# Sparse graph attention with feed-forward: the software pipeline one step shorter, its lead-in written out, attention edges dealt by a computed pace

## What is computed

```python
hs, ht = layer_norm(x), layer_norm(h_target)            # scale and bias ln1
q = (ht @ Wq + bq) / sqrt(32);  k = hs @ Wk + bk;  v = hs @ Wv + bv
logits = where(adj != 0, q . k per head, -1e30)
ctx = softmax(logits) @ v                               # over the sources of each target
ht = layer_norm(ht + ctx @ Wo + bo)                     # scale and bias ln2
ff = gelu(ht @ W1) @ W2                                 # 256 -> 1024 -> 256
out = layernorm(x + ht + ff)                            # no scale
```

## Time and profile before

| | |
|---|---|
| median of 3 runs | 333.95 us (333.85 to 336.05) |
| profiled execution, its time | 333.58 us |
| its span in the profile | 331.8 us, 4310 instructions |
| PE busy | 250.6 us (76%) |
| DVE busy | 223.1 us (67%) |
| POOL busy | 186.1 us (56%) |
| ACT busy | 157.6 us (47%) |
| last third of it, chain that ended last | DVE and PE by turns |

### The profile page before, as it was taken

The page is one execution under the profiler, slowest core; times in us unless marked ns, Lnnn a source line. Parts: engine busy times, 40 slices in busy tenths (PEclk is TensorE's granted clock), DMA queues, the critical chain, the costliest instruction groups (busy, mean ns, idle before and its releaser), DMA issues.

```text
span 331.8 us, 4310 instructions
## 1 busy us (share of the span) xinstructions
PE 250.6 (76%) x1383; PEld 195.3 (59%) x1383; DVE 223.1 (67%) x623; ACT 157.6 (47%) x282; POOL 186.1 (56%) x204
## 2 busy tenths in 40 slices
PE   6599895650216745979999899899895796949990
PEld 6344331210112524967999799789784695939980
DVE  3489879798825437367897698688885589780111
ACT  1656999610014323465767567746752244303220
POOL 8776522390077765725777888887878603111211
PEclk9789979875555565979999999999999599787996
DMA  6999999999546645424346564454565700000000
GB/s 159 401 396 418 418 391 328 355 303 333 207 131 185 191 132 169 143 64 126 113 147 171 159 174 144 132 166 147 161 174 168 155 28 16 18 0 16 16 17 24
DMA packets 23490, 58.04 MB, mean 175 GB/s; under 512 B 4051, under 2 KB 12517, under 8 KB 21414
## 3 DMA queue, kind: packets, MB, share of 16 engines
q0 software_dynamic: 8400, 27.01, 28.1%
q1 hardware_dynamic: 14228, 29.91, 24.7%
q10 hardware_dynamic: 834, 0.79, 1.1%
HBM read 51.40 MB, written 10.49 MB: 187 GB/s over the span
## 4 chain that ended last, share of the span: by engine, by line
PE 28%; POOL 26%; issue 17%; DVE 15%; ACT 9%; DMA 2%; another core or an unknown queue 1%; POOLq 0%; ACTq 0%; DVEq 0%
POOL arena L746 12%; PE score L984 8%; PE bank L993 7%; PE bank L854 4%; POOL rstd_late L772 4%; POOL tab L736 3%; DVE arena L1599 2%; DVE arena L1640 2%; DVE logits L1601 2%; POOL out_dram L778 2%; ACT arena L1174 2%; PE bank L962 2%; DVE arena L1646 2%; ACT query L1182 2%; ACT arena L1165 1%
## 5 line engine op out<-in xcount | busy, mean ns | idle before, releaser
L746 POOL DMA_INDIRECT arena<-kv_scratch,places x79 | 82.7, 1047 | 22.5 <-issue 22.5
L984 PE MATMUL score<-h_t,w_sb 128*128 128x128 f32 x512 | 66.3, 286 | 2.0 <-ACT h_t L1299 2.0
L984 PEld LDWEIGHTS score<-h_t,w_sb 128*128 128x128 f32 x512 | 64.9, 203 | 3.4 <-ACT h_t L1299 2.6
L993 PE MATMUL bank<-w_sb,gelu_t 128*128 128x256 f32 x256 | 62.1, 395 | 5.4 <-issue 4.8
L993 PEld LDWEIGHTS bank<-w_sb,gelu_t 128*128 128x128 f32 x256 | 50.3, 200 | 13.5 <-issue 5.4
L1245 ACT ACTIVATE gelu_t<-score 128x512 f32<-128x512 f32 x32 | 19.1, 597 | 68.2 <-PE score L984 51.2
L772 POOL TENSOR_TENSOR rstd_late<-var_late,minus_half 128x2 f32<-128x2 f32 (+2 forms) x22 | 22.2, 1009 | 34.6 <-DVE var_late L1711 24.3
L778 POOL DMA_INDIRECT out_dram<-y_out,places x16 | 17.1, 1071 | 34.0 <-ACT y_out L1291 30.8
L854 PE MATMUL bank<-tab,arena 128*128 128x512 f32 x64 | 32.9, 668 | 0.8 <-DVE arena L1423 0.4
L1599 DVE TENSOR_TENSOR arena<-arena,query 128x1024 f32<-128x1024 f32 (+3 forms) x22 | 24.6, 1116 | 7.9 <-ACT query L1276 6.5
L1676 DVE SCALAR_TENSOR_TENSOR y_sum<-bank,place_value,tab 128x256 f32<-128x256 f32 x16 | 7.7, 480 | 30.4 <-PE bank L998 29.2
(11 more groups left out here) (153 smaller groups left out, 447.2 us busy)
## 6 DMA issues: line engine op xcount, KB each, us to landing
arena<-in_adj_dram SPq DMA_DIRECT2D x6, 1024.0 KB, 11.8
w_sb<-in_adj_dram SPq DMA_DIRECT2D x6, 1024.0 KB, 12.9
kv_scratch<-arena SPq DMA_DIRECT2D x8, 512.0 KB, 9.7
tab<-in_x_dram SPq DMA_DIRECT2D x4, 512.0 KB, 11.0
own_t<-in_adj_dram SPq DMA_DIRECT2D x2, 1024.0 KB, 14.8
gelu_t<-in_adj_dram SPq DMA_DIRECT2D x2, 1024.0 KB, 11.4
tab_scratch<-in_L_gnn_h_target_dram SPq DMA_DIRECT2D x1, 2048.0 KB, 12.0
tab_scratch<-in_x_dram SPq DMA_DIRECT2D x1, 2048.0 KB, 16.5
```

Of the source, the lines that this page charges most:

```text
L746: pool.indirect_dma_start(kv_ring[:, ring_at[m] + j, :], None, kv_dram[:, :], at).then_inc(gathered[m][piece], 16)
L984: mm = pe.matmul(hid_ps[(2 * n + half) % 3][:, f % 4 * P:(f % 4 + 1) * P], w1_sb[:, k, f * P:(f + 1) * P], h2_t[:, n % 2, k, :], start=(k ...
L993: pe.matmul(ff_ps[:, 0:D], gelu_t[:, n % 2, f, :], w2_sb[:, f, :], start=(f == 0), stop=False, skip_group_check=True)
```

## The change

- `LEAD_KEYS`, `LEAD_VALUES`: keys of tiles 0 to 2 and values of tiles 0 and 1 are weighed ahead of step 0, in a list written out (`lead()` on DVE, `lead_fetches` on POOL, first branches of `finish` on PE and ACT). Each of own tiles 0 to 4 and residual 0 has its own group of moments there. Own tile 4 is only normalised in the lead-in and turned in step 0; own tiles 5 and 6 and all other edges belong to steps from 0 on.
- PE projects tile s+1 in step s, right behind mlp_in(s, 0), where before it was tile s+2 at the step's end. turn_h2(s+1) stands between the halves of mlp_out(s), turn_context(s+2) at the end.
- The own tiles' steps are a list, `OWN_STEP`. `may_use` lets keys be weighed two or three steps behind their own tile. Stretches are dealt evenly over steps 0 to 13, and a step's stretches are cut in three (`parts_of`): first (up to 3.0 units) ahead of the moments, second (one stretch) between moments and shift, rest behind the shift. ACT's exponentials follow the same parts: first between the two gelus, second behind gelu 1, rest behind copy_h2.
- Worked out from these formulas, the deal is 9.7 units in the lead-in, then 4.4, 5.0, 5.0, 11.9, 6.2, 14.3, 7.4, 8.1, 9.7, 7.7, 5.7, 8.3, 8.8, 8.2 in steps 0 to 13; gathers: 14 in the lead-in, then 6, 7, 7, 6, 11, 6, 7, 7, 6, 7, 6, 5 in steps 0 to 11.
- All own rows are gathered from `tab_scratch`, x with them; `fetch_x` goes.
- The matmuls against the identity in `project_out` and `add_h2` become transposes (`is_transpose=True`).

The diff, cut to its core:

```diff
-    EDGES_LEAD = 3
-    RAMP = 0.35
-    DIRECT = 2
-    CONTEXT_LATE = 1
-    RAMP_ROWS, STEP_ROWS = 3, 6.5
+    STEP_ROWS = 6.5
+    FIRST_WORK = 3.0
+    OWN_STEP = [-5, -4, -3, -2, -1, 0, 0, 1, 2, 2, 3, 4, 5, 6, 7, 8]
...
+        def may_use(stretch, step):
+            stage, m, a, _ = stretch
+            return stage == VALUES or step >= OWN_STEP[m] + 2 + own_work[OWN_STEP[m]].index(m)
+        LEAD_KEYS, LEAD_VALUES = 3, 2
+        lead_part = [w for w in stretches if w[1] < (LEAD_KEYS if w[0] == KEYS else LEAD_VALUES)]
+        stretches = [w for w in stretches if w not in lead_part]
         all_work = sum(work_in(w) for w in stretches)
...
+        for step in range(0, TILES + 1):
+            target = all_work * min(1.0, (step + 1) / (TILES - 2))
...
+            while stretches and may_use(stretches[0], step) and (
+                    any(w[1] <= step + (2 if w[0] == VALUES else 3) for w in stretches) or
+                    work_done + work_in(stretches[0]) / 2 < target):
...
+        lead_fetches = [(0, -1), (0, 0), (0, 1), (1, -1), (ROOT, 0), (2, -1), (1, 0), (ROOT, 1), (1, 1), (3, -1), (ROOT, 2),
+                        (2, 0), (2, 1), (4, -1), (ROOT, 3), (3, 0), (ROOT, "res"), (3, 1), (ROOT, 4), (3, 2)]
...
@@ project_out and add_h2 on PE
-                              stop=False, skip_group_check=True)
+                              stop=False, is_transpose=True, skip_group_check=True)
...
@@ finish on PE, steps from lo on
+                    mlp_in(s, 0)
+                    if s + 1 < hi and not first:
+                        project_out(s + 1)
                     if own_now:
                         turn_own(own_now[0])
+                    if first:
+                        turn_context(1)
+                    mlp_in(s, 1)
+                    if own_now:
+                        project_query(own_now[0])
+                    if first:
+                        project_out(1)
+                    mlp_out(s, 0)
+                    if len(own_now) > 1:
+                        turn_own(own_now[1])
+                    if s + 1 < hi:
+                        turn_h2(s + 1)
+                    mlp_out(s, 1)
+                    add_h2(s)
+                    if len(own_now) > 1:
+                        project_query(own_now[1])
+                    if lo == 0 and s + 2 < hi:
                         turn_context(s + 2)
...
@@ finish on ACT
                         gelu(s, 0)
                     for o in own_now[:1]:
                         copy_own(o)
...
+                    exponentials(first)
+                    if s < hi:
                         gelu(s, 1)
+                    for o in own_now[:1]:
+                        copy_query(o)
+                    for o in own_now[1:]:
+                        copy_own(o)
+                    exponentials(second)
+                    if s + 1 < hi:
                         normalise_res(s + 1)
+                        copy_h2(s + 1)
+                    exponentials(rest)
                     if s > lo:
                         normalise_y(s - 1)
...
@@ DVE
+            def lead():
...
+                own_stats(0)
+                make_shift(("lead", 0))
+                own_stats(1)
+                make_shift(("lead", 1))
+                own_stats(2)
+                weigh_keys(0, 0, SLOTS[ORDER[0]])
+                make_shift(("lead", 2))
+                sum_tally()
+                weigh_values(0, 0, SLOTS[ORDER[0]])
+                own_stats(3)
+                weigh_keys(1, 0, SLOTS[ORDER[1]])
+                make_shift(("lead", 3))
+                take_stats(("lead", "res"), [], 0, None)
+                set_flag()
+                make_shift(("lead", "res"))
+                weigh_values(1, 0, SLOTS[ORDER[1]])
+                own_stats(4)
+                weigh_keys(2, 0, SLOTS[ORDER[2]])
+                make_shift(("lead", 4))
...
                     if s > lo:
                         add_x(s - 1)
+                    weigh_edges(first)
                     if key in group_at:
                         take_stats(key, [own_of(lo + m) for m in own_work[s - lo]],
                                    s + 1 if lo <= s + 1 < hi else None, s - 1 if s > lo else None)
...
+                    weigh_edges(second)
                     if key in group_at:
                         make_shift(key)
...
+                    weigh_edges(rest)
```

More of the change, by code:

```diff
@@ L477, in graph_attention, with parts_of @@
[L477 to L481 removed]
+        assert not stretches
+        def parts_of(step):
+            some, first, second = list(edge_work[step]), [], []
+            while some and sum(work_in(w) for w in first) + work_in(some[0]) / 2 <= FIRST_WORK:
+                first.append(some.pop(0))
+            if some:
+                second.append(some.pop(0))
+            return first, second, some
```

218 lines of the change are left out of this document (104 added, 114 removed).

## The result

| kernel, chip | time, us (median, lowest to highest) | kernel before on that chip | ratio, 95% interval |
|---|---|---|---|
| changed, first chip | 329.06 (328.34 to 330.69) | 333.9 | 0.985 [0.980, 0.990] |
| changed, again, another chip | 328.37 (326.81 to 330.20) | 331.79 | 0.994 [0.990, 0.998] |

The change makes the kernel faster by 1.5% on one chip and 0.6% on another. I had forecast 3.9%. Medians are of all executions, ratios of those outside the chip's second, slower state. The profiled execution after has a span of 329.0 us, where its neighbours have 326.6 to 327.7; the second profile ("again") has 325.1.

The account below looks back on a forecast made before the run. Latency in the lead-in, POOL in steps 1 to 10, PE at the end; 130.6 + 136.3 + 21.0 + 15.6 + 8.1 = 311.6, + 5 (clock) + 3 (unnamed waits) = 319.6, + 1.8 = 321 us; range 311 to 330.

Parts of the forecast that it names:

- the sum's 21.0 us for steps 12 and 13: Steps 12 and 13 take 11.0 + 10.0 us against 30.2 before, as turn_context moves behind mlp_out: 9 us gained.
- the loop of steps 1 to 11: Closed loop through edge work, root, shift, h, turning and mlp_out: 136.3 us against 130.6 before, clock and unnamed waits apart.
- Rival 4: Lead-in not shorter: something unseen holds the start of step 0 near 130, giving 334 us; chance 0.04.
- Plain transposes and table loads: Identity matmul pairs on PE take 0.38 us, not 0.61; ScalarE has 27 table loads instead of 23, 1.28 us each.
- PE's clock: Waits of 3 to 6 us ahead of turn_h2 in steps 4, 5, 6, 9 halve PE's clock: +5 us.
- Rival 3: PE's clock drops in the seven other steps too, 3 us each, 21 us in all: 342 us; chance 0.09.
- h 0.6: Loop term for steps 1 to 11: h takes 0.6 us behind the shift, ahead of its turning on PE.
- gelu 1 would end at T + 7.5 ... hidden, by about 1 us: ScalarE's second gelu, counted from PE's step start T, ends before PE wants it at T + 8.2 to 9.
- rival 6: ScalarE's gelu 1 comes 2.8 us later, so PE waits 1.5 us in about six steps: 330 us; chance 0.04.
- Rival 5: POOL's first drain, behind step 11's scatter, delays the root after it: +4, 325 us; inside the forecast's own range (0.61).
- Unnamed waits: ScalarE's waits that no engine ended, 15.2 us before and mostly hidden by POOL: +3 us, bounds 0 and 8.
- Rival 2: Loop tighter than counted: steps 1 to 11 each 1 us longer from late gathers or roots, 332 us; chance 0.10.

Follow-up runs that it names:

- late turning: Changed kernel with PE's turning of h for step s+1 behind both halves of mlp_out and add_h2, not between the halves: 317.24 us, 0.964 of the kernel before.
- the even one: Changed kernel with a deal in which a step takes no further stretch when half of it would lead over 9.0 units: 317.12 us, 0.963 of the kernel before.
- the swap: Changed kernel with ScalarE's copy of the second own tile behind the normalisation of h, not ahead of it: 326.44 us, 0.985 of the kernel before.
- the drain moved: Changed kernel with POOL's drains behind the step's root and ahead of the next scatter, the first one step later: 322.92 us, 0.972 of the kernel before.

## Why the prediction went wrong

The direction was right, the gain less than half of the forecast. The step that failed most is the sum's 21.0 us for steps 12 and 13, which had nothing for the drain: they took 28.3. The other is the loop of steps 1 to 11, which took 149.6 us where 144.3 had been allowed. The profiled span is 329.0 against 319.6 by the sum; the differences are -2.5 (step 1 starts at 128.05, not 130.6), +5.3 (steps 1 to 11, beyond the 8 allowed), +7.3 (steps 12 and 13), +0.5 and -1.1 (end and tail).

- **Lead-in and step 0: right.** 39.6 us from the first gather to step 1, forecast 40.1. Its two parts were each off: step 0 began 22.7 us (24.8 in "again") behind the first gather, not 26.5, and took 16.8 (13.3), not 13.6. That the two cancel in the first profile is luck. The first gather alone came 2.0 us sooner, which need not be an effect of the change: it lies between 88.4 and 90.8 in the traces of all kernels, and at 90.5 and 89.8 in the two of the kernel before. Rival 4 is out.
- **Plain transposes and table loads: right.** 0.38 us for a pair that accumulates; 13 + 14 = 27 loads. The Trainium skill's drain with each switch ("ScalarE: Activation LUTs", What ACT_TABLE_LOAD costs) is not in these traces: in the rows above gelu starts 0.01 us behind the end of its load.
- **PE's clock: right in kind and size.** In steps 3, 5, 6, 10 of the first profile mlp_out behind the wait ran at half clock, 5.5 us in sum; I had put 5 (but in steps 4, 5, 6 and 9). Rival 3 (in each step) is out: the granted clock is 0.95 from 128 on. The waits themselves were larger: 34.3 us of PE ahead of the turning of h, of which late turning filled 22.
- **Steps 5 and 6: right** (14 and 16 forecast, 16.3 and 17.0 measured, of which 1.4 each is the clock I had counted apart). The uneven deal lengthened step 6 (14.0 with the even one, 15.9 in "again"), not step 5, which stayed at 17.2.
- **Steps 1 to 3: a step that failed.** They took 43.2 us in the first profile and 41.6 in "again", for 35.0. What failed is "h 0.6" behind the shift, and "gelu 1 would end at T + 7.5 ... hidden, by about 1 us". Gelu 1 ends at T + 8.6 in step 3 of "again" (T + 10.9 in the first profile), and ScalarE copies the query and the second own tile before h. My loop had VectorE, POOL and PE in it, ScalarE not; 6.5 us in the first profile, 6.1 in "again", in steps 1, 2 and 3 alone. This is rival 6's mechanism by another cause: the order of ScalarE's queue, where I had looked for the price of a load. Step 3 of the first profile has the unnamed wait below and 1.2 us of clock on top. That this lag sets the total isn't shown: the swap took 2.7 us off it, and the time did not move.
- **Step 10.** 12.0 forecast, 15.0 measured, 1.5 of it the clock. Root 10 is 4.6 us behind its variance, with the gathers of the rows above ahead of it, two of them held by VectorE. I had priced a gather at the 1.33 us of the earlier trace rows, where it took (89.5 + 22.3)/79 = 1.42.
- **Step 12: the step that failed most.** The sum had no term for the drain. Rival 5 had the mechanism and the place, but a price of 4 us, taken from the 4.7 that root 11 was late in the earlier trace rows. Root 12 was 7.3 us late, and the wait made PE's clock fall as well: 17.6 us for 11.0. Without the drain the step took 10.8. I had read 8.93 us of idleness as partly slack; it is all the drain's, 0.084 us for each of some 107 indirect DMAs, and nothing of it depends on what waits.
- **Unnamed waits: right in size.** +3 forecast; one cost about 2 us in step 3 of the first profile (ScalarE 4.55 us, VectorE 2.05), one of 3.76 at 220.50 about 1 us: step 7 takes 12.8 us there, and 11.8 with the drain moved or with ScalarE's swap, whose traces have none in it.
- **The signs.** A mean over 13.5 us in steps 1 to 11 was named as a sign of being wrong; it is 13.6 in the first profile and 13.4 in "again". The first step began before 122, and the clock stayed over 0.85. Rival 2 (late gathers, 1 us in each step) had the right engine: POOL's root is 2.5 to 5.2 us late in steps 4, 5, 8, 9 and 10, part of which the loop had counted.
- **Slips that move nothing.** The gain in the lead-in and step 0 was 146.86 - 130.6 = 16.3 by the forecast's own terms, not 17, and POOL's step before 10.9 to 11.8, not 11.3.

## To carry to other kernels

When a pipeline is made shorter, write the closed loop with every engine's queue in it, the one that seems idle too: here h stood behind ScalarE's queue for 6 us in three steps. A wait of an in-order engine can be filled by moving work that stands behind it ahead of it. An uneven deal can cost more than its excess: here it also lengthened the wait of the shift and the time at half clock. Count the indirect DMAs ahead of a drain, and put the drain where nothing on the path stands behind it.

## What the runs showed of the hardware

- POOL carries a debt of 0.084 us for each indirect DMA of 128 rows, paid at the next drain. In the kernel without drains in its steps that is the one at the end of the program: 9.7 us between the last scatter and the end, with no bytes moving in the last 5.7 of them. What it consists of is open.
- With only 8 to 26 of them since the last drain, a drain right behind a gather left POOL idle for 3.2 to 3.7 us.
- Indirect DMAs on POOL are held while VectorE runs an operation on two inputs from SBUF, and take about 0.8 us from its end on; 26 became 7 when the products had one input. The Trainium skill ("SBUF — State Buffer", Who interferes with whom) says that such an operation shuts out a GpSimd instruction that reads SBUF, and that it was not seen to slow the generation of descriptors. This trace agrees with the first, as these DMAs read their row numbers from SBUF. It differs from the second: begun inside such a product they took up to 2.30 us, in place of 0.95 to 1.01.
- The kernel before took 328.8, 331.0, 331.8, 333.9, 334.7 and 334.8 us on different chips or occasions, 1.8% apart.
